# Output buffers six deep and gathered rows five deep in a fused attention and mixture-of-experts kernel

## What is computed

```python
x = x + attention(layernorm(x), ctx)                  # keys and values: ctx and x itself
xf = layernorm(x).reshape(T, h)                       # T = 2048 tokens
topk_w, topk_idx = top_k(softmax(xf @ gate_w.T), 6)   # 64 experts, 6 per token
buf_tok, buf_w = ...                                  # up to 128 tokens of each expert
gx = xp[buf_tok]                                      # gather, (64, 128, 512)
g, u = split(einsum('ech,ehi->eci', gx, gate_up_proj))
eo = einsum('eci,eih->ech', silu(g) * u, down_proj) * buf_w[..., None]
routed = zeros.at[buf_tok].add(eo)                    # scatter-add
shared = silu(xf @ shared_gate_w.T) * (xf @ shared_up_w.T) @ shared_down_w.T
x = x + routed + shared
```

## Time and profile before

| What | us |
|---|---|
| Median of three executions | 825.71 |
| The three executions | 825.69, 825.71, 830.84 |
| The profiled execution, its own time | 825.93 |
| Its span (first to last instruction) | 824.2 |

### The profile page before, as it was taken

How to read it: one execution, slowest core, us unless ns; L and a number is a source line. 1 busy time by engine, 2 the same in 40 slices (tenths; PEclk the granted TensorE clock), 3 DMA queues, 4 the chain that set the end, 5 groups by cost and what they waited for, 6 DMA issues and landing times.

```text
span 824.2 us, 10919 instructions
## 1 busy us (share of the span) xinstructions
PE 771.6 (94%) x3886; PEld 655.5 (80%) x3886; DVE 591.1 (72%) x1168; ACT 455.0 (55%) x801; POOL 311.7 (38%) x258
## 2 busy tenths in 40 slices
PE   6999999999999999999998999998999989878982
PEld 5888878888788887888877887897978878767871
DVE  6537576675587665863696998998988989876820
ACT  3433333442334313342345898998888989766720
POOL 1001010455005640156105455555665655655523
PEclk9999999999999999999999999999999999998997
DMA  4962153332712326202746999999999999999778
GB/s 162 319 230 86 71 217 138 104 103 73 275 61 103 107 111 243 103 30 87 288 180 186 350 330 344 324 345 360 307 336 345 341 334 331 342 321 321 153 128 162
DMA packets 50676, 180.34 MB, mean 219 GB/s; under 512 B 7664, under 2 KB 8048, under 8 KB 37872
## 3 DMA queue, kind: packets, MB, share of 16 engines
q1 hardware_dynamic: 31120, 137.64, 44.2%
q0 software_dynamic: 19504, 42.02, 23.5%
HBM read 143.33 MB, written 44.97 MB: 228 GB/s over the span
## 4 chain that ended last, share of the span: by engine, by line
PE 44%; POOL 15%; issue 15%; DMA 11%; DVE 8%; ACT 4%; SPq 1%; POOLq 0%; DVEq 0%; ACTq 0%
PE bank L1097 8%; PE bank L1099 8%; PE bank L1098 7%; POOL xg L1324 5%; POOL out_rows L1332 5%; POOL second_sum L1332 4%; DMA stage<-wvT_in 3%; PE scores L1097 3%; PE scores L1099 3%; PE scores L1098 3%; DMA out_rows<-eo,idx_all 3%; PE bank L905 2%; DMA second_sum<-eo,idx_all 2%; DMA out_rows<-product,idx_all 2%; PE bank L1076 1%
## 5 line engine op out<-in xcount | busy, mean ns | idle before, releaser
L1456 DVE TENSOR_TENSOR gu_lo<-raw,gu_hi 128x768 fp32r<-128x768 f32 x128 | 122.3, 957 | 30.9 <-ACT gu_hi L1376 26.1
L421 POOL DMA_INDIRECT table<-rows,slot x72 | 80.5, 1119 | 157.7 <-DVEq L832 114.1
L1376 ACT ACTIVATE gu_hi<-raw 128x768 fp32r<-128x768 f32 x128 | 107.2, 840 | 11.7 <-DMA raw<-expert_in 11.7
L1097 PE MATMUL ps_gu<-gu_hi,xgT_hi 128*128 128x384 f32 x256 | 94.2, 368 | 1.3 <-DVE xgT_lo L1456 1.3
L1324 POOL DMA_INDIRECT xg<-x_rows,idx_all x64 | 71.6, 1118 | 60.8 <-DVEq L668 27.0
L1099 PE MATMUL ps_gu<-gu_hi,xgT_lo 128*128 128x384 f32 x256 | 88.7, 346 | 0.0
L1098 PE MATMUL ps_gu<-gu_lo,xgT_hi 128*128 128x384 f32 x256 | 88.7, 346 | 0.0
L449 ACT ACTIVATE qT<-bank 128x512 fp32r<-128x512 f32 x32 | 19.2, 599 | 113.1 <-PE bank L1099 104.2
L454 ACT ACTIVATE pbuf<-scores,negmax 128x1024 f32<-128x1024 f32 x16 | 17.9, 1117 | 69.0 <-DVE negmax L603 69.0
L581 DVE TENSOR_TENSOR qT<-bank,qT 128x512 fp32r<-128x512 f32 x32 | 22.1, 689 | 45.6 <-ACT qT L449 36.8
L1097 PEld LDWEIGHTS ps_gu<-gu_hi,xgT_hi 128*128 128x128 f32 x256 | 50.3, 196 | 1.8 <-DVE xgT_lo L1456 1.7
(11 more groups left out here) (273 smaller groups left out, 2224.7 us busy)
## 6 DMA issues: line engine op xcount, KB each, us to landing
raw<-expert_in SPq DMA_DIRECT2D x64, 1024.0 KB
rest<-rest_in SPq DMA_DIRECT2D x32, 256.0 KB
x_rows<-pbuf SPq DMA_DIRECT2D x17, 256.0 KB, 2.1
stage<-wkT_in SPq DMA_DIRECT2D x4, 1024.0 KB
stage<-ctxT_in SPq DMA_DIRECT2D x4, 1024.0 KB
stage<-wvT_in SPq DMA_DIRECT2D x4, 1024.0 KB
stage<-ctx_in SPq DMA_DIRECT2D x4, 1024.0 KB
stage<-woT_in SPq DMA_DIRECT2D x4, 1024.0 KB
```

Of the source, the lines that this page charges most:

```text
L421: pool.indirect_dma_start(out=table, out_offset=bass.IndirectOffsetOnAxis(ap=slot[:, i, k:k + 1], axis=0), in_=rows[:, i, k, :], in_offset ...
L1097: pe.matmul(out, still[0], moving[0], start=first, stop=False)
L1376: act.activation(gu[n % GU_SLOTS][0][part], gate_up_of(n, part), ACT.Copy).then_inc(weights_high, 1)
L1456: return dve.tensor_tensor(lo, x, hi.bitcast(F32), ALU.subtract)
```

## The change

`eo` gets six slots: `products[0]` and a tile that was unused space (`above_raw3`, now `eo_above`) come in addition. `xg` gets five slots: two tiles of unused space are added (`xg_below`, `xg_above`). Scaling of set r waits for the add of set r-6. The gather of expert e waits until PE has transposed expert e-5, and POOL issues the gather of expert e+9 ahead of the add of expert e, where it was e+7. In the lead, gathers 3 and 4 wait for nothing on PE.

```diff
--- before.py
+++ after.py
@@ -1105,7 +1105,8 @@
 RAW = 4
 GU_SLOTS = 2
 DN_SLOTS = 3
-EO = 4
+EO = 6
+XG = 5
 
 
 PAIRS = [(b, m) for b in (0, B - 1, *range(1, B - 1)) for m in range(3)]
@@ -1186,16 +1187,16 @@
     rest = [sb(f"rest{n}", [P, D]) for n in range(2)]
     gu = [(halves(sb("gu_hi0", [P, GU], F32R)), halves(sb("gu_lo0", [P, GU], F32R)))]
     raw.append(sb("raw2", [P, ROW]))
-    sb("above_raw2", [P, D])
+    xg_below = sb("xg_below", [P, D])
     gu_hi1 = sb("gu_hi1", [P, GU], F32R)
-    sb("above_gu_hi1", [P, D])
+    xg_above = sb("xg_above", [P, D])
     ssilu, shid, products = [], [], []
     for to, name in ((ssilu, "ssilu"), (shid, "shid")):
         for n in range(2):
             sb(f"above_{name}{n}", [P, 3 * D])
             to.append(sb(f"{name}{n}", [P, D])[:, :])
     raw.append(sb("raw3", [P, ROW]))
-    sb("above_raw3", [P, D])
+    eo_above = sb("eo_above", [P, D])
     dn_lo2 = sb("dn_lo2", [P, D], F32R)
     gu_lo1 = [sb("gu_lo1_0", [P, HALF], F32R)[:, :]]
     silu = [sb("silu0", [P, KB])]
@@ -1207,11 +1208,12 @@
         sb(f"above_product{n}", [P, above * D])
         products.append(sb(f"product{n}", [P, D])[:, :])
     kept.products = products
-    xg = sb("xg", [P, 3, D])
+    xg_here = sb("xg", [P, 3, D])
+    xg = [xg_here[:, n, :] for n in range(3)] + [xg_below[:, :], xg_above[:, :]]
     hid = sb("hid", [P, 2, HP])
     hidT = sb("hidT_hi", [P, 2, HP], F32R), sb("hidT_lo", [P, 2, HP], F32R)
     eo_more = sb("eo", [P, 2, D])
-    eo = products[2:4] + [eo_more[:, n, :] for n in range(2)]
+    eo = products[2:4] + [eo_more[:, n, :] for n in range(2)] + [products[0], eo_above[:, :]]
     xgT = sb("xgT_hi", [P, 2, D], F32R), sb("xgT_lo", [P, 2, D], F32R)
     dn.append((sb("dn_hi2", [P, 2 * D], F32R), dn_lo2))
     ident, tab, idx_all = kept.ident, kept.tab, kept.idx_all
@@ -1224,7 +1226,7 @@
 
     raw_loaded = [sem(f"raw_loaded{n}") for n in range(RAW)]
     rest_loaded = [sem(f"rest_loaded{n}") for n in range(2)]
-    gathered = [sem(f"gathered{n}") for n in range(3)]
+    gathered = [sem(f"gathered{n}") for n in range(XG)]
     weights_high = sem("weights_high")
     weights_split = sem("weights_split")
     xgT_full = sem("xgT_full")
@@ -1319,10 +1321,10 @@
         def gather(e):
             if e >= E:
                 return
-            if e >= 3:
-                pool.wait_ge(xgT_full, e - 2)
-            pool.indirect_dma_start(out=xg[:, e % 3, :], out_offset=None, in_=x2_rows,
-                                    in_offset=index(("expert", e))).then_inc(gathered[e % 3], 16)
+            if e >= XG:
+                pool.wait_ge(xgT_full, e - XG + 1)
+            pool.indirect_dma_start(out=xg[e % XG], out_offset=None, in_=x2_rows,
+                                    in_offset=index(("expert", e))).then_inc(gathered[e % XG], 16)
 
         def add_rows(what):
             r = SET_NO[what]
@@ -1341,12 +1343,13 @@
         pool.wait_ge(kept.sum_cleared, 32)
         gather(3)
         add_rows(("shared", (0, 0)))
-        gather(4)
-        gather(5)
+        for e in range(4, 7):
+            gather(e)
         add_rows(("shared", (0, 1)))
-        gather(6)
+        gather(7)
+        gather(8)
         for e in range(E):
-            gather(e + 7)
+            gather(e + 9)
             add_rows(("expert", e))
             if e in EVENT_AT and EVENT_AT[e][0] == "down":
                 add_rows(("shared", EVENT_AT[e][1]))
@@ -1407,7 +1410,7 @@
             r = SET_NO[what]
             act.wait_ge(dn_full, r + 1)
             if r >= EO:
-                act.wait_ge(added[r % 2], (r // 2 - 1) * 16)
+                act.wait_ge(added[r % 2], ((r - EO) // 2 + 1) * 16)
             scale = tab[:, what[1], 1:2] if what[0] == "expert" else 1.0
             act.activation(eo[r % EO], ps_dn[:, r % 2, :], ACT.Copy, scale=scale).then_inc(eo_ready, 1)
 
@@ -1569,11 +1572,11 @@
         last.then_inc(dn_full, 1)
 
     def rows(pe, e):
-        pe.wait_ge(gathered[e % 3], e // 3 * 16 + 16)
+        pe.wait_ge(gathered[e % XG], e // XG * 16 + 16)
         if e:
             pe.wait_ge(xgT_low, e)
         for c in range(C):
-            last = pe.transpose(ps_xgT[:, cols(c)], xg[:, e % 3, cols(c)], ident[:, :])
+            last = pe.transpose(ps_xgT[:, cols(c)], xg[e % XG][:, cols(c)], ident[:, :])
         last.then_inc(xgT_full, 1)
 
     def gate_up(pe, e):
```

## The result

| | before | after |
|---|---|---|
| median of 20 executions | 827.69 us | 823.18 us |
| ratio, with 95% interval | | 0.995 (0.9929 to 0.9971) |
| profiled execution, its own time | 825.93 us | 828.62 us |
| span | 824.2 us | 826.9 us |

The change saves 0.5%, or 4.1 us, which is under the 1% that this text counts as a change, though its interval leaves out 1. One execution of the kernel before took 1553.03 us and is not in the ratio; without it the median before is 827.29 us. The forecast was 821.6 us, or 4.3 us less than the profiled 825.9. The profiled execution of the changed kernel was one of its longer ones, over the median by more than the whole effect.

What follows compares the result with a forecast made beforehand. It took the two chains of adds as the bound from about 500 to 776 us. Terms -1.7 - 3.2 + 0.6 = -4.3 us took the profiled 825.9 to 821.6 us, range 816.0 to 828.0.

Steps and rivals of the forecast that it cites:

- What bounds the stage: Experts' stage, about 500 to 776 us: two chains of adds bind, 4.67 us an add against PE's 4.17 a set.
- The gain at the end: Last adds: 1.7 us from no longer waiting for ACT, 3.2 us from weight loads running out 9.3 us sooner.
- The cost in the crowded stretch: While PE wins its lead, its extra DMA demand slows adds: 0.6 us lost, chosen between nothing and 5.7 us.
- The tail: Merges and four adds after the last add: bytes stay, gain taken as nothing, at most 2.7 us.
- PE's lead: Experts' stage: six slots let ACT and PE run two more sets ahead, 9.3 us, won in full by some 590 us.
- the check on ACT's waits: New profile: ACT's waits for adds fall from 21.3 to some 12 us and begin near 590 us, not 506.
- The rows: Gathers nine ahead keep PE's wait for gathered rows at about 0.8 us, under 3 us in the new profile.
- DMA as the bound: Crowded stretch: DMA, not the adds' order, limits; only moving 1.0 MB out helps, about 3.0 us, 822.9 us; chance 0.14.
- The lead passed through whole: Late adds speed up to 2.6 us each and follow ACT; the end moves by 9.3 us to 816.6; chance 0.12.
- stalls-are-jitter rival: Two more slots swallow PE's stalls, PE keeps its free pace, and 24.2 us go: 801.7 us; chance 0.06.
- The slower rival: Faster weight loads make adds land later; at 10.0 us a parity cycle, in place of 9.34, 838 us; chance 0.12.
- My own sign of being wrong: Prediction fails if the adds' pace changes either way, each 1% being 2.4 us, or PE comes to wait for rows.

Runs made afterwards that it cites:

- The kernel with the reload moved: Against the changed kernel, the shared expert's late 2 MB reload was split into two 1 MB transfers, issued 24 and 12 experts earlier; 823.23 us, ratio 0.9968.
- second profile of before: The kernel before, unchanged, run once more for one execution; 826.2 us.
- second profile of the change: The changed kernel, with nothing altered, run once more; 824.62 us, ratio 0.997 to the kernel before.

## Why the prediction was right

**What bounds the stage** held. Two chains of adds, each waiting for its own landings, set the pace: a third chain brought the ratio from 0.995 to 0.9793. The pace was 4.67 and 4.66 us an add before the change, and 4.77 and 4.68 after it.

**The gain at the end** held in place and size. The two terms, 1.7 and 3.2 us, were both to fall into the last adds, 4.9 us together. The last eleven adds took 37.7 and 36.6 us with four slots and 32.6 and 32.2 us with six, which is 4.7 us between the means. The other kernels with loads of one DMA agree: 41.4 us with four slots, 33.8 and 32.3 with six. The split into the two terms was not measured. The larger one was worked out from the lead of 9.3 us, and that lead was not reached, so the agreement of the total with 4.9 us is partly luck.

**The cost in the crowded stretch**, forecast at 0.6 us, is not well measured. It was 1.1 us over the 52 adds in one pair of profiles (0.02 an add) and 5.4 us in the other (0.10), so both lie above the forecast. The kernel with the reload moved, with 241.7 us, shows no cost. The first pair of profiles alone would have suggested a cost that eats the whole gain. The interval of the ratio, a gain of 2.4 to 5.9 us, agrees with a cost near 0.6 us if the end gives 4.7, but the term was a choice between 0 and 5.7 us, and that it fits is luck as much as reading. Why one execution had 4.77 stays open; executions of one kernel lie over 10 us apart here.

**The tail carries the last add one to one**: 31.7 and 31.5 us from merges to end before, 32.1 and 32.0 after, 32.0 with two DMAs (782.26 to 814.3) and 32.0 with three chains (778.08 to 810.1).

**PE's lead was mis-sized.** I took two whole sets, 9.3 us. Over 55 steps it measured 292.0 - 288.2 = 3.8 us in the first pair of profiles and 291.4 - 284.9 = 6.5 us in the second. At the last expert's set it was less than nothing in the first (787.68 against 785.79) and 6.1 us in the second (780.02 against 786.08). With it fell the check on ACT's waits: I said 12 us in place of 21.3, and they are 23.2 in one profile and 10.1 + 4.0 + 2.9 + 0.8 + 0.6 = 18.4 in the other (15.1 + 4.7 + 3.0 + 1.7 = 24.5 in the second profile of before). The moment at which the slots are full first was near what I said (590 said; 600 and 629 seen). What failed is the step from a lead to waits: once the slots are full again, the waits return. The end time did not need the full lead where the last adds waited for landings and not for ACT, as they did in the second profile of the change.

**The rows** behaved as said: PE's wait for them stays small, 0.3 us and 1.2 us in the two profiles, and is 17.0 us if the gathers are left seven ahead.

**The baseline** moved under the forecast. The three executions it stood on had a median of 825.71 us, and all twenty have 827.69. The forecast saving of 4.3 us is close to the measured 4.1, and 821.6 us is 1.6 us below the measured 823.18 mostly for that reason.

**The rivals.** DMA as the bound had 822.9 us, nearer to 823.18 than my own 821.6, so the time alone could not reject it; the runs do. As it was put it is wrong: 344 GB/s was no ceiling, since three chains held 354 over 250 us with the same bytes for each expert. The 366 GB/s at which it would have bitten were not held in any run, and the longer landings with three chains (12.3 us against 9.3) suggest that DMA is the next bound. The lead passed through whole (816.6 us) did not happen: the last eleven adds took 2.96 and 2.93 us each, not 2.6, and the lead was smaller. The stalls-are-jitter rival fails, since more slots did not remove the waits. The slower rival did not happen in the median. In the first profile of the change, though, a cycle took 2 x 4.77 = 9.55 us, just past the 9.53 from which the change was to lose, and that execution did take longer than the profiled one of before (828.62 against 825.93). My own sign of being wrong, a change of the adds' pace, thus showed in one profile of two, by 2%.

## What to carry to other kernels

When an engine waits for a buffer whose consumer is a chain of ordered transfers, compare the chain's pace with the producer's before adding buffers. If the chain is slower, more buffers move the producer ahead once, and the gain shows only where the load thins out at the end. Look then at what makes one link slow. Here issuing each weight load of another queue as two smaller DMAs sped the links up, and two DMAs in place of one, with the old slots, gave more than the slots did (0.9859 against 0.995). And two buffers in one loop have to grow together, or the wait moves from one to the other.

## What the runs showed that I had not expected

- At the same bytes for each expert and nearly full DMA engines (share 1.04 to 1.06), moving an expert's 1024 KB in two DMAs with 4 KB runs raised the stretch from 333 and 342 GB/s (the two profiles of the change) to 349 GB/s and took the 52 adds from 4.77 and 4.68 us each to 4.40 (507.3 to 735.9 us). Four DMAs with 2 KB runs gave 342 GB/s, and ACT waited 21.2 us for weights.
- A share of 1.04 did not mean that no more could be moved: three chains reached 354 GB/s at 1.05.
